# Linear-attention feature stage of a graph layer on one Trainium2 core: one factor of the feature products read from PSUM, and transposes moved behind the main sums

## The reference, cut to what matters

```python
kn = _normalize(k) * scale
vN = v1 / N
kv_mod = jnp.einsum('bhni,bhnj,bhne->bhije', kn, kn, vN)
kv = jnp.einsum('bhnd,bhne->bhde', kn, vN)
vsum = jnp.sum(vN, axis=-2)[:, :, None, :]
```

## Time and profile before

| what | value |
|---|---|
| median of three runs | 3498.53 us (3497.65 to 3501.57) |
| the profiled execution | 3492.37 us |
| its span | 3490.6 us |
| DVE busy over the span | 2384.7 us, 68% |
| PE busy | 2597.5 us, 74% |
| POOL busy | 2218.2 us, 64% |
| ACT busy | 1241.4 us, 36% |

### The profile page before, as it was taken

The page is one execution under the profiler, slowest core; times in us unless marked ns, Lnnn a source line. Parts: engine busy times, 40 slices in busy tenths (PEclk is TensorE's granted clock), DMA queues, the critical chain, the costliest instruction groups (busy, mean ns, idle before and its releaser), DMA issues. The chain is left out here.

```text
span 3490.6 us, 52008 instructions
## 1 busy us (share of the span) xinstructions
PE 2597.5 (74%) x12153; PEld 1706.2 (49%) x12153; DVE 2384.7 (68%) x5282; ACT 1241.4 (36%) x2631; POOL 2218.2 (64%) x2128
## 2 busy tenths in 40 slices
PE   4888876878878787787878778787863509999930
PEld 2444443545444444444444444444542508888830
DVE  7999996777767777676777767677768813222258
ACT  1333324444545444454544445444431102222210
POOL 2777776777777777777777777777775652222210
PEclk9999997889889898988989989898975559999975
DMA  5111113444444444544444444444441247777743
GB/s 145 29 32 29 31 31 108 134 137 134 132 139 129 138 133 133 140 128 140 137 131 135 135 135 132 131 134 130 137 133 38 76 155 236 231 234 235 235 148 121
DMA packets 305258, 453.64 MB, mean 130 GB/s; under 512 B 117079, under 2 KB 206148, under 8 KB 305017
## 3 DMA queue, kind: packets, MB, share of 16 engines
q0 software_dynamic: 87024, 243.45, 25.4%
q1 hardware_dynamic: 187469, 135.23, 13.5%
q10 hardware_dynamic: 30540, 72.47, 5.9%
HBM read 395.75 MB, written 56.83 MB: 130 GB/s over the span
## 5 line engine op out<-in xcount | busy, mean ns | idle before, releaser
L930 POOL DMA_INDIRECT rows_g<-node_rows,idx x1568 | 1610.0, 1027 | 490.2 <-issue 477.4
L1145 PE MATMUL p_m<-msg,sel 128*128 128x264 f32 x3520 | 1061.0, 453 | 246.0 <-DVE msg L1116 149.1
L1145 PEld LDWEIGHTS p_m<-msg,sel 128*128 128x128 f32 x3520 | 732.6, 219 | 389.3 <-issue 258.3
L1116 DVE TENSOR_TENSOR msg<-rows_g,msg 128x1024 f32<-128x1024 f32 x440 | 537.2, 1221 | 84.9 <-ACT msg L1024 65.6
L1024 ACT ACTIVATE msg<-lg 128x32 f32<-128x32 f32 x440 | 100.3, 228 | 957.3 <-DVE lg L1110 822.6
L1725 POOL DMA_INDIRECT moe<-ysb,token x128 | 123.6, 966 | 374.8 <-DVE ysb L1713 353.4
L1162 PE MATMUL p_scr<-q_t,sel_sum 32*128 32x512 f32 x832 | 254.8, 683 | 127.6 <-ACT qfeat L1000 127.5
L1106 DVE TENSOR_TENSOR lg<-rows_g,ends 128x32 f32<-128x32 f32 x440 | 84.8, 193 | 370.0 <-SPq L951 275.8
L987 ACT ACTIVATE sel_t<-apart,ones 128x512 bf16<-128x512 bf16 x443 | 319.8, 722 | 31.2 <-issue 1.0
L1047 DVE TENSOR_TENSOR sel<-iota_bf,dst_t 128x512 f32<-128x512 bf16 x441 | 304.8, 691 | 24.3 <-issue 6.0
L984 ACT ACTIVATE apart<-dst_all,iota_neg 128x512 bf16<-128x512 bf16 x443 | 313.2, 707 | 8.5 <-DMA dst_all<-dst_bc 8.1
(11 more groups left out here) (310 smaller groups left out, 3338.2 us busy)
## 6 DMA issues: line engine op xcount, KB each, us to landing
dst_all<-dst_bc ACTq DMA_DIRECT2D x112, 512.0 KB, 4.3
wa<-in_L_ffn_w_dram SPq DMA_DIRECT2D x64, 512.0 KB, 3.7
wb<-in_L_ffn_w_dram SPq DMA_DIRECT2D x64, 512.0 KB, 4.8
rows_g<-node_rows,idx POOLq DMA_INDIRECT x1568
xs<-slot_x SPq DMA_DIRECT2D x64, 258.0 KB, 3.5
ya<-moe SPq DMA_DIRECT2D x48, 256.0 KB, 3.0
bb<-in_L_ffn_b_dram SPq DMA_DIRECT2D x64, 128.0 KB, 4.9
qs<-qn_dram ACTq DMA_DIRECT2D x14, 512.0 KB, 6.3
```

The costliest lines, as they stand in the source:

```text
L930: pool.indirect_dma_start(rows_g[:, j, u, :], None, node_rows, bass.IndirectOffsetOnAxis(ap=idx[q][:, j, u:u + 1], axis=0)).then_inc(gathe ...
L1116: dve.tensor_tensor(m4, g3[:, :, 0:D].rearrange("p u (h e) -> p u h e", h=H), msg[j % 2][:, :, D:ROW].unsqueeze(3).broadcast_to([P, TC, H, ...
L1145: mm = pe.matmul(p_m[j % 2][:, 0:ROW], sel[j][:, u, :], msg[j % 2][:, u, :], start=(u == 0), stop=(u == TC - 1))
```

## The change

ACT gets one more instruction per tile: behind `k_ready` and ahead of `km` it copies the 256 scaled keys from SBUF into a new PSUM bank `p_k` and raises `keys_out`. DVE's products read their broadcast factor from `p_k` and the shifted one from SBUF as before; they wait for `keys_out`. POOL's products still read SBUF for both. To free a bank, `p_t` and `p_v` become the halves of one bank `p_tv`: so `turn(t + 1)` now waits for `qkv_taken` of tile t, and PE's order in a tile is projections, `sums_main(t - 2)`, the turn, `sums_tail(t - 2)`. The turned sums behind the loop go to `p_k` in place of `p_v`.

```diff
-        def products(eng, feat, wrapped, u):
+        def products(eng, feat, keys, wrapped, u):
 
             base = wrapped[:, u, 0:1]
             whole = [base.ap[0][0], P]
-            return eng.tensor_tensor(feat.rearrange("p (d i) -> p d i", i=C),
-                                     bass.AP(base.tensor, base.offset, [whole, [0, DIAGS - 1], [1, C]]),
+            return eng.tensor_tensor(feat.rearrange("p (d i) -> p d i", i=C), keys.unsqueeze(1).broadcast_to([P, DIAGS - 1, C]),
                                      bass.AP(base.tensor, base.offset, [whole, [1, DIAGS - 1], [1, C]]), ALU.mult)
...
-            p_t = ps("p_t", [P, 512], c)
+            p_tv = ps("p_tv", [P, 512], c)
+            p_t, p_v = p_tv[:, 0:D], p_tv[:, D:2 * D]
+            p_k = ps("p_k", [P, 512], c)
...
-            p_v = ps("p_v", [P, 512], c)
...
                     act.wait_ge(k_ready, t + 1)
+                    act.copy(p_k[:, 0:D].rearrange("p (h e) -> p h e", h=H), kk[s][:, :, 0:C]).then_inc(keys_out, 1)
                     act.activation(km[s][:].rearrange("p (h e) -> p h e", h=H), kk[s][:, :, 0:C], ACT.Copy,
                                    scale=mask[s][:]).then_inc(masked, 1)
...
-                def sums(t, s):
+                def sums_main(t, s):
                     pe.wait_ge(masked, t + 1)
                     pe.wait_ge(dve_feats, t + 1)
                     pe.wait_ge(pool_feats, t + 1)
+                    for u in range(H):
+                        add_sum(p_main[u // 4][(u % 4) * C:(u % 4 + 1) * C, :], vm[s][:, u * C:(u + 1) * C], feat[s][:, u, :])
+
+                def sums_tail(t, s):
                     for g in range(2):
                         add_sum(p_tg[g][:, GK:GK + P + 1], km[s][:, g * P:(g + 1) * P], k1[s][:, g, :])
-                        add_sum(p_tg[g][:, 0:GK], vm[s][:, g * P:(g + 1) * P], tail1[s][:, g, :])
-                    for u in range(H):
-                        mm = add_sum(p_main[u // 4][(u % 4) * C:(u % 4 + 1) * C, :], vm[s][:, u * C:(u + 1) * C], feat[s][:, u, :])
+                        mm = add_sum(p_tg[g][:, 0:GK], vm[s][:, g * P:(g + 1) * P], tail1[s][:, g, :])
                     mm.then_inc(summed, 1)
...
                     mm.then_inc(projected, 1)
+                    if not (isinstance(t, int) and t < 2):
+                        sums_main(t - 2, s)
                     if not (isinstance(t, int) and t == T - 1):
+                        pe.wait_ge(qkv_taken, t + 1)
                         turn(t + 1, 1 - s)
                     if not (isinstance(t, int) and t < 2):
-                        sums(t - 2, s)
+                        sums_tail(t - 2, s)
...
                 def features(t, s, units):
                     for u in units:
-                        a = products(dve, feat[s][:, u, :], kk[s], u)
+                        a = products(dve, feat[s][:, u, :], p_k[:, u * C:(u + 1) * C], kk[s], u)
                     return a
...
                     if not first:
                         wait(dve, summed, t - 2)
+                        wait(dve, keys_out, t)
                         features(t - 1, 1 - s, (0, 1))
...
                 dve.wait_ge(summed, T - 2)
+                dve.wait_ge(keys_out, T)
                 features(T - 1, 1, range(KV_UNITS)).then_inc(dve_feats, 1)
...
-                        products(pool, feat[s][:, u, :], kk[s], u)
+                        products(pool, feat[s][:, u, :], kk[s][:, u, 0:C], kk[s], u)
```

More of the change, by code:

```diff
@@ L567, in gps_layer @@
             k_ready = sem("k_ready", c)
+            keys_out = sem("keys_out", c)
             masked = sem("masked", c)
@@ L660, in body @@
                     wait(pe, qkv_taken, t)
-                    for o, lo, hi in ((p_row[:, 0:W_Q], 0, W_Q), (p_qk[:], W_Q, W_Q + 2 * D), (p_v[:, 0:D], W_Q + 2 * D, W_Q + 3 * D)):
+                    for o, lo, hi in ((p_row[:, 0:W_Q], 0, W_Q), (p_qk[:], W_Q, W_Q + 2 * D), (p_v, W_Q + 2 * D, W_Q + 3 * D)):
                         for kc in range(2):
@@ L664, in body @@
                     mm.then_inc(projected, 1)
+                    if not (isinstance(t, int) and t < 2):
+                        sums_main(t - 2, s)
                     if not (isinstance(t, int) and t == T - 1):
+                        pe.wait_ge(qkv_taken, t + 1)
                         turn(t + 1, 1 - s)
                     if not (isinstance(t, int) and t < 2):
-                        sums(t - 2, s)
+                        sums_tail(t - 2, s)
                 turn(0, 0)
                 ring_peeled(pe, T, 2, body)
-                sums(T - 2, 0)
-                sums(T - 1, 1)
+                for t in (T - 2, T - 1):
+                    sums_main(t, t % 2)
+                    sums_tail(t, t % 2)
                 pe.wait_ge(sums_ready, 1)
@@ L679, in _ @@
                 for m in range(FCH):
-                    mm = pe.transpose(p_v[:, m * P:(m + 1) * P], tg_sb[m // 2][:, (m % 2) * P:(m % 2 + 1) * P], ident[:])
+                    mm = pe.transpose(p_k[:, m * P:(m + 1) * P], tg_sb[m // 2][:, (m % 2) * P:(m % 2 + 1) * P], ident[:])
                 mm.then_inc(main_turned, 1)
@@ L712, in body @@
                     dve.tensor_copy(mask[s][:], vmask[:, bass.ds(t, 1)])
-                    dve.tensor_tensor(v[s][:], p_v[:, 0:D], b_qkv[:, 2 * D:3 * D], ALU.add).then_inc(qkv_taken, 1)
+                    dve.tensor_tensor(v[s][:], p_v, b_qkv[:, 2 * D:3 * D], ALU.add).then_inc(qkv_taken, 1)
                     if not first:
                         wait(dve, summed, t - 2)
+                        wait(dve, keys_out, t)
                         features(t - 1, 1 - s, (0, 1))
@@ L751, in _ @@
                 for g in range(2):
-                    a = dve.scalar_tensor_tensor(out=w_far[:, g, :], in0=p_v[:, 2 * g * P:(2 * g + 1) * P], scalar=A_COEF / 2, in1=head_ones[:],
+                    a = dve.scalar_tensor_tensor(out=w_far[:, g, :], in0=p_k[:, 2 * g * P:(2 * g + 1) * P], scalar=A_COEF / 2, in1=head_ones[:],
                                                  op0=ALU.mult, op1=ALU.mult)
@@ L755, in _ @@
                 for g in range(2):
-                    dve.scalar_tensor_tensor(out=w_lin[:, g, :], in0=p_v[:, (2 * g + 1) * P:(2 * g + 2) * P], scalar=SCALE ** 2 * B_COEF,
+                    dve.scalar_tensor_tensor(out=w_lin[:, g, :], in0=p_k[:, (2 * g + 1) * P:(2 * g + 2) * P], scalar=SCALE ** 2 * B_COEF,
                                              in1=head_ones[:], op0=ALU.mult, op1=ALU.mult)
```

## The result

Four executions of the changed kernel took 3411.79 to 3425.63 us, median 3417.48; the kernel before, with one more run beside them, 3498.94. The ratio is 0.9768, 95% interval 0.9747 to 0.9789: 81 us less. The profiled execution has a span of 3416.1.

A forecast was written before the change was run, and what follows sets the result against it. DVE was taken to set the pace at 9.19 us a tile, falling to 7.57: 79.4 us over 49 tiles plus 2.4 at the end, 81.8 off the 3498.5 median, gives 3416.7; own range 3408 to 3426, eight-in-ten range 3400 to 3440.

The forecast's parts named there:

- K: Zero point of the predicted times: the end of DVE's line 738, where a tile ends.
- first product: DVE's first product of a tile: starts at 1.26 or 1.61 us, behind lines 711 to 713.
- old line 725: DVE's line 725: starts at 5.17 or 5.25 us, costs 0.16 and not 0.36, as POOL is done by then.
- ACT's copy: ACT's copy into PSUM: 0.46 us, hidden by 0.7 of lines 711 to 713; uncovered, 22 us in all.
- The hold: DVE and POOL hold each other's instructions; with one factor in PSUM, DVE's two products take 1.21 us, not 2.22 or 1.73.
- The PSUM price: DVE's product with its broadcast factor from PSUM: taken at 0.60 to 0.61 us, by line 711.
- the slower case: Rival: the repeated PSUM read costs DVE's product a second cycle per element; 9.8 us a tile, time 3528; chance 0.05.
- The remaining hold: DVE's line 721, both inputs in SBUF, still waits for POOL's third product, ending 0.03 us behind it at 4.03 or 4.11.
- POOL's tail: POOL's product of 256 at the tile's end: 0.57 us, then a 0.40 copy; POOL done at 4.9 to 5.0.
- sum of its parts: PE's work a tile: tail sums 1.51, main sums 1.85, projections 3.39, turn 0.42; 7.17 us of 7.57.
- The clock: Rival: PE's clock goes on falling, 11.5 falls at 1.25 us make 14 us, time 3431; chance 0.18.
- The end: Behind the loop: POOL's last tile start to the last sums takes 4.95 us in place of 7.31, 2.36 saved.

## Why the prediction was right

The forecast was 3416.7, the median is 3417.5. The mechanism holds, and so does its size: 81.8 us were to be saved, the stage's work ends 80.8 sooner. That the number is off by less than 1 us is luck all the same. The four executions lie 14 us apart, and the profiled one was put at 3410.6 and took 3417.9, because the later stages took 6 us more in it; it was also taken to lie 6.1 below the median, and lies 0.4 above it. Some terms were mis-sized without reaching the path, as told below. Step by step, in times from K:

| step | predicted | measured |
|---|---|---|
| first product | 1.26 / 1.61 | 302.87 - 301.61 = 1.26; 1.61 in the other tile (310.82 - 309.21) |
| end of old line 721 | 4.11 / 4.03 | 4.11 / 4.04 |
| old line 725 | 5.25, 0.16 long | 5.24, 0.16 long |
| next K | 7.61 / 7.53 | 7.60 / 7.51 |
| tile, mean | 7.57 | 7.55 |
| products on DVE, on POOL | 0.69, 1.14 | 0.681, 1.147 |
| ACT's copy | 0.46 in a row, hidden | 0.31 in a row, hidden |

- **The hold.** That a two-input instruction of DVE escapes POOL's hold once one input is in PSUM was inferred from one row, line 711 at an even 692. The run with the line undone and the run without POOL's products show it from both sides, and the run with two heads of five shows both prices in one kernel.
- **The PSUM price.** The fixed surcharge on a PSUM source that the Trainium skill's table gives (VectorE: DVE Perf Modes, section on the TRN2 errata) would have made each product 65 ns longer by my estimate. The 250 products with a PSUM factor have a median of 681 ns, against 684 with both in SBUF and POOL quiet: in this form no surcharge of that size shows, and the row decided rightly. The repetition of 32 elements, the slower case's ground, costs nothing either.
- **The remaining hold.** Not freed, as said: 0.46 to 0.93 in place of 0.18. It was put at 0.5 a tile on the path, and taking it away gave 0.42.
- **POOL's tail.** It was priced like `qst`, 0.57, and takes 0.67 (305.66 to 306.33), so POOL is done at K + 5.12 (306.73) and not at 4.9 to 5.0. Line 734 starts 0.12 behind that: the term was too small by 0.1 and stayed off the path by little. That thin margin is why this line is held in the runs above, where DVE comes earlier or POOL has more to do.
- **PE.** The sum of its parts was near, 7.17 against 7.04 where PE became the bound, but two parts were too dear and one too cheap, and the errors cancel. From the loads of that run (`ss_scale` in PSUM, head 4 on POOL):

```profile
298.72 0.16 PEld L642 LDWEIGHTS p_main<-acc,vm 128*32 128x32 f32 x8 [0.33 <-issue]
...
300.57 0.14 PEld L647 LDWEIGHTS p_tv<-ident,xn 128*128 128x128 f32 x1 [0.84 <-issue]
...
300.74 0.30 PEld L642 LDWEIGHTS p_tg<-k,km 128*128 128x128 f32 x2
...
301.95 0.86 PEld L669 LDWEIGHTS p_row<-w_cat,xt 128*128 128x128 f32 x4
...
305.75 0.16 PEld L642 LDWEIGHTS p_main<-acc,vm 128*32 128x32 f32 x8 [0.33 <-issue]
```

  The main sums take 1.85, as said, the turn 0.17 and not 0.42, the tail 1.21 and not 1.51, the projections 3.80 and not 3.39. In the changed kernel 2.00 lie between the main sums and the turn, because the turn waits for `v` in every tile: its load starts 0.21 behind the end of the line for `v` (302.96 to 303.17), where 0.07 was reckoned. PE stands 0.08 or 0.43 for it, in turn, and 0.37 ahead of the main sums in every second tile: 0.44 a tile in all, and some 0.4 was forecast. The projections were done at K + 6.81 (307.39 + 1.03 in PE's timeline), 0.3 sooner than predicted, and the slack was larger.
- **The clock.** The rival in which it goes on falling had 0.18. The granted clock stayed at its upper level, 2.4 GHz, through all tiles, and PE was busy for 283 of the 300 us from 100 to 400, where it had been busy for 249. It still fell right behind the loop, at 446.0, outside what was counted:

```profile
424.40:427.80 3.40, 3.40 (x17) 2.52 (x16) 3.33 (x7) 1.64 (x5) 3.27 (x5) 1.00 0.42 79
...
442.60:446.00 3.40, 1.16 (x12) 0.50 (x16) 2.57 (x9) 0.71 (x2) 0.84 (x3) 1.00 0.00 0
446.00:449.40 3.40, 3.40 (x15) 1.91 (x8) 3.40 (x6) 0.11 (x1) 3.40 (x4) 0.50 0.14 43
```

  In front of that fall PE was busy 1.16 of 3.40 us, where the earlier trace rows had 1.49; within the loop it was 3.2 on average, and 3.40 in the first of these lines. The stage's mean of 0.99 is by that end alone. In the kernel with the SBUF factor back, 34 us of the loop were at the lower level again, as before the change, so the falls go with PE's idle time. They did not set the tile there: in its steady part every step was 8.81 or 9.59 in turn, to within 0.02, with a fall in it or without.
- **The end.** The last main sums load at 450.41, 5.07 behind POOL's start of its last tile (445.34), where 4.95 was said; the 0.1 is POOL's tail again. So 2.2 us were saved in place of 2.36. DVE's wait of 0.51 for `p_k` ends at 445.77, beside it, as said.

## What to carry to other kernels

When instructions of one form have a wide spread on VectorE and GpSimd, and the minimum of one equals that of a neighbour with a PSUM operand, look first for the two engines holding each other; a run without one engine's instructions settles it. The price after the change can then be read off that neighbour: here, moving one factor to PSUM gave 1.63 us a tile for a copy of 0.31 on an engine with time to spare. Small instructions are held too, here up to 0.75 us for one of 16 elements (0.93 in place of 0.18), so look for them next. And a bank freed by sharing puts a new wait on the engine that writes it: place that wait where work stands before it and behind it.

## What the runs showed that I had not expected

- The hold does not need a second tensor input: a `tensor_scalar` of 16 elements with one SBUF input took 0.156 to 0.175 us in the changed kernel and 0.66 to 0.68 in the steady tiles with POOL's tail ahead of it. The Trainium skill (SBUF — State Buffer, section on who interferes with whom) counts `tensor_scalar` among the operations that can enter a mode in which they contend with GpSimd, if their operands meet its conditions. That it is held, the runs show; whether by that mode, no run here tells. Work moved to POOL paid for it: 0.60 taken off DVE gave 0.10.
- Two transposes between two groups of sums cost PE 0.16 to 0.17 us from load to load, or 0.24 to 0.28 from matmul to matmul, against 0.42 read from loads ahead of an idle time.
- ACT copies 256 elements into PSUM in 0.376 us on average. Beside each other, in the run with two more copies, one to SBUF took 0.403 and one to PSUM 0.368; from start to start both cost 0.31.
